# TensorE's sampling program as a loop of two chunks, over a ring of 16 image rows twice, with each step's terms in three parts

## The chip, the cores and the metric

The kernel runs on one core of a Trainium2 chip. The core's engines run side by side and wait for each other through semaphores: TensorE (PE, matmul), VectorE (DVE), ScalarE (ACT), GpSimd (POOL) and SyncE (SP, which here issues nearly all DMAs). The metric is the device time of one execution in microseconds (us), lower is better. Before the change the median of 3 runs is 777.53 us (776.26 to 784.17).

## What is computed

A first layer (channel norm, three 1x1 convolutions, windowed attention, a gate, a residual) ahead of a deformable 3x3 convolution with batch norm, relu and residual, all in fp32 on an array of 8 x 16 x 64 x 64. The change is in the second layer alone:

```python
om = conv3x3(x, w_off) + b_off               # 27 channels
off_y, off_x, mask = om[:, :9], om[:, 9:18], sigmoid(om[:, 18:])
py = off_y + row + ky;  px = off_x + column + kx      # for each of 9 taps
sampled = bilinear(x, py, px) * mask         # zero outside the image
out = einsum("bckhw,ock->bohw", sampled, w) + b
out = relu(batchnorm(out)) + x
```

## The kernel before, in words

The bilinear sample is written as two hat functions. `img4` holds the image already multiplied by each tap's weights: for a column on the partitions, 9 taps x rows x 16 outputs. A matmul with the hat of the horizontal distance as its weights (`wt`, 64 x 64 for one row and tap) picks the columns; a product with the hat of the vertical distance (`aw`) over NR = 7 rows around the pixel and a sum over 9 x 7 = 63 terms pick the rows. Rare larger offsets go another way, that the change does not alter in kind.

Two images lie side by side on the 128 partitions, so the 8 images are PAIRS = 4 passes g over NCH = 8 chunks c of 8 image rows: 32 chunks s, each of SPC = 4 steps, 128 steps n in all, two output rows a step. A step runs through all engines:

- SP loads px of the step, for the chunk ahead, from a scratch array in DRAM, the same 4,608 bytes to 64 partitions and twice (`load_px`, 288 KB each); it waits for `wt_ready` of the step whose place is overwritten.
- ScalarE makes Abs and Relu of it (`hats`) into one of two halves of `wt`.
- TensorE does 40 matmul calls of 64 x 64 (`taps`), in two halves of 512 and 496 columns (32 and 31 of the 63 terms) into 6 of the 8 PSUM banks, two a half, three deep. Each call of an fp32 matmul is two weight loads and two matmuls in the trace.
- VectorE multiplies each half with `aw` (`product`, L886), and sums what is left two steps later (`add`, L897).
- GpSimd folds the 63 terms to 23 (L595, L598), and prepares `aw` (L557, L565) once a chunk.

Between the steps, four times a chunk, stand smaller jobs of TensorE: in rounds of 3, 3 and 2 rows the weighted image rows of the next pass (`slot_round`, read out by ScalarE in `slots_out`), and in the first 16 chunks the offsets of the other pairs (`offsets` at the even chunks, `to_samples` at the odd ones; VectorE's `coordinates` and `peak` belong to them). `img4` holds all 64 rows and a border; a round for chunk s writes the rows that the pass before has done with, so the first pass's rows (7 chunks, `first`) are made ahead of the loop, while offsets of the first pairs are computed.

All programs are written out: TensorE's 32 chunks stand one behind the other, 6,083 matmul calls from the end of the attention loop to the end. The attention stage of the first layer is a loop on TensorE of two times four steps, run three times.

## Time and profile before

| | us |
|---|---|
| median of 3 runs | 777.53 |
| the profiled execution | 782.31 |
| its span, first to last instruction | 780.5 |
| sampling loop, first product to last | 471 |
| share busy: TensorE, its weight loads, VectorE, ScalarE, GpSimd | 79%, 60%, 75%, 66%, 66% |
| moved by DMA | 93.08 MB, 119 GB/s in the mean |

How the rows further down are read: PE is TensorE's matmuls, PEld its weight loads, L with a number a line of the kernel. Busy time is in us with the number of instructions behind it; a few per cent of the matmul records are missing. In a row of waits, "A <- B: 53.2, 38, 3.6" says that A stood idle 53.2 us in 38 pieces of up to 3.6 us until B was done; "issue" is idle time in which nothing that the profile shows was waited for. In a window's row the mean granted share of TensorE's clock (1.00 is 2.4 GHz) stands behind the engines, then the mean busy share of the 16 DMA engines, then GB/s.

### The profile page before, as it was taken

To read this page: it belongs to the slowest core of one execution; us is meant where nothing else is said; L and a number is where in the kernel's file an instruction comes from. 1 tells how busy PE (TensorE), PEld (TensorE's weight loads), DVE (VectorE), ACT (ScalarE), POOL (GpSimd) and SP (SyncE) were. 2 spreads that over 40 slices of the span, in tenths; PEclk is the share of its full clock that TensorE was granted. 3 is DMA by queue.
4 is the path that set the end of the run, shared out by engine and by line. 5 is a ranking of instruction groups with operands and counts; after the bars stand their busy time and mean duration, and the time that the engine had idled before them with its cause. 6 is when DMAs were issued, how large, how long until landed. Compare 5 with 4: busy or idle time off the path is not lost. (4 is left out here: it accounts for less than half of the span.)

```text
span 780.5 us, 31804 instructions
## 1 busy us (share of the span) xinstructions
PE 616.7 (79%) x13528; PEld 466.2 (60%) x13528; DVE 585.8 (75%) x782; ACT 518.3 (66%) x826; POOL 511.7 (66%) x469
## 2 busy tenths in 40 slices
PE   4989999996899898897798688778877767677632
PEld 1335666664345576776676666667766657576532
DVE  3477877786422287998988798889998889879935
ACT  2656676675123596977877687859878687768514
POOL 4036444551331088998979798969989898889920
PEclk9999999998799998999999999999999998879956
DMA  4000000000166277877868676737658878967102
GB/s 180 1 0 2 1 1 0 0 0 2 43 147 146 61 193 186 201 177 187 202 153 199 146 186 156 184 99 190 180 135 190 196 151 174 204 161 191 36 3 107
DMA packets 41747, 93.08 MB, mean 119 GB/s; under 512 B 21647, under 2 KB 21775, under 8 KB 41360
## 3 DMA queue, kind: packets, MB, share of 16 engines
q1 hardware_dynamic: 39762, 90.58, 47.6%
q8 instruction: 104, 1.70, 1.0%
q10 hardware_dynamic: 1854, 0.58, 0.3%
q14 instruction: 27, 0.22, 0.1%
HBM read 79.47 MB, written 3.28 MB: 106 GB/s over the span
## 5 line engine op out<-in xcount | busy, mean ns | idle before, releaser
L1300 PE MATMUL PS<-region 64*64 64x112 f32 (+5 forms) x11184 | 393.5, 268 | 90.0 <-issue 63.5
L1300 PEld LDWEIGHTS PS<-region 64*64 64x64 f32 (+2 forms) x11184 | 314.9, 141 | 138.2 <-issue 97.5
L886 DVE TENSOR_TENSOR region<-PS,region 128x1024 f32<-128x1024 f32 (+1 forms) x256 | 298.9, 1203 | 57.8 <-PE PS L1300 53.2
L595 POOL TENSOR_TENSOR region<-region 128x960 f32<-128x960 f32 x128 | 239.8, 1873 | 50.2 <-DVE region L886 50.0
L1148 ACT ACTIVATE region<-region 128x1152 f32<-128x1152 f32 x128 | 149.1, 1165 | 53.8 <-PE PS L1300 44.3
L1145 ACT ACTIVATE region<-region,cst 128x1152 f32<-128x1152 f32 x128 | 159.3, 1245 | 7.1 <-DMA region<-px_scratch 7.1
L598 POOL TENSOR_TENSOR region<-region 128x320 f32<-128x320 f32 x128 | 117.5, 918 | 10.0
L897 DVE TENSOR_REDUCE region<-region 128x32 f32<-128x736 f32 x128 | 116.2, 908 | 0.0
L1300 PE MATMUL PS<-wg,xp 64*64 64x144 f32 x1024 | 82.7, 291 | 8.9 <-issue 5.9
L1300 PEld LDWEIGHTS PS<-wg,xp 64*64 64x64 f32 x1024 | 64.6, 137 | 17.9 <-issue 12.3
L518 POOL TENSOR_TENSOR region<-region,cst 128x512 f32<-128x512 f32 x32 | 33.8, 1056 | 63.3 <-PE PS L1387 58.7
L1164 ACT ACTIVATE region<-PS 128x432 f32<-128x432 f32 (+1 forms) x75 | 35.6, 479 | 39.9 <-PE PS L1300 39.8
L557 POOL TENSOR_TENSOR region<-x,cst 128x504 f32<-128x504 f32 x32 | 34.3, 1071 | 28.3 <-ACT region L1262 16.3
L1072 ACT ACTIVATE region<-PS 128x512 f32<-128x512 f32 x32 | 19.1, 596 | 35.9 <-PE PS L1395 35.9
L565 POOL TENSOR_TENSOR region<-region 128x504 f32<-128x504 f32 x32 | 34.0, 1061 | 11.1 <-ACT region L1183 11.1
L1300 PE MATMUL PS<-region,woff 96*64 96x512 f32 x120 | 33.2, 595 | 1.5 <-DVE xp L824 0.8
L716 DVE RECIPROCAL region<-PS 128x16 f32<-128x16 f32 x32 | 8.3, 258 | 30.2 <-PE PS L1300 30.2
L1253 ACT ACTIVATE region<-PS 128x432 f32<-128x432 f32 (+1 forms) x21 | 10.3, 490 | 28.7 <-PE PS L1300 28.2
L743 DVE SCALAR_TENSOR_TENSOR PS<-region,wr,PS 128x504 f32<-128x504 f32 (+3 forms) x40 | 29.0, 725 | 0.0
L1395 PEld LDWEIGHTS PS<-cst,region 128*128 128x128 f32 x160 | 16.9, 140 | 18.4 <-issue 14.2
L1395 PE MATMUL PS<-cst,region 128*128 128x128 f32 x160 | 24.3, 282 | 2.6 <-ACT region L1078 2.1
L1300 PE MATMUL PS<-region,bd 128*128 128x512 f32 x48 | 24.0, 624 | 1.1 <-ACT region L1034 1.0
(141 smaller groups left out, 655.2 us busy)
## 6 DMA issues: line engine op xcount, KB each, us to landing
region<-px_scratch SPq DMA_DIRECT2D x256, 288.0 KB, 4.9
out<-region SPq DMA_DIRECT2D x4, 512.0 KB, 3.0
cst<-in_consts SPq DMA_DIRECT2D x1, 1102.5 KB, 8.7
x<-in_x SPq DMA_DIRECT2D x1, 1024.0 KB, 10.7
two<-xp SPq DMA_DIRECT2D x14, 64.0 KB, 3.4
px_scratch<-two SPq DMA_DIRECT2D x48, 18.0 KB
...
```

Source lines behind the costliest of these rows:

```text
L518: pool.tensor_tensor(ks[:, u, :, 0:4 * K1].rearrange("p w (b k) -> p w b k", b=4), kw[:, bass.ds(n * 2 * K1, 2 * K1)].rearrange("p (w k) - ...
L557: pool.tensor_tensor(aw4[:, rows], py4[:, rows, bass.ds(g, 1), :].rearrange("p r g k -> p (r g) k").unsqueeze(3).to_broadcast([P, RPC, KK, ...
L565: pool.tensor_tensor(aw4[:, rows], aw4[:, rows], mk4[:, rows, bass.ds(g, 1), :].rearrange("p r g k -> p (r g) k").unsqueeze(3).to_broadcas ...
L595: pool.tensor_tensor(two_rows[:, :, :, 0:NA - FOLD], two_rows[:, :, :, 0:NA - FOLD], two_rows[:, :, :, FOLD:NA], ALU.add).then_inc(half_re ...
L598: pool.tensor_tensor(two_rows[:, :, :, 0:FOLD - KEEP], two_rows[:, :, :, 0:FOLD - KEEP], two_rows[:, :, :, KEEP:FOLD], ALU.add).then_inc(f ...
L886: v.tensor_tensor(uu[:, 2 * u:2 * u + 2, :, lo:hi], PS[:, banks:banks + 2, 0:(hi - lo) * C].rearrange("p h (a o) -> p h o a", o=C), awf[:, ...
L897: v.tensor_reduce(totals(2 * (n % STEPS), n // STEPS), uu[:, b:b + 2, :, 0:KEEP], AX.X, ALU.add).then_inc(os_ready, 1)
L1145: a.activation(rows, rows, ACT.Abs, bias=c_("negx")).then_inc(ab_ready, 1)
L1148: a.activation(wt[:, i % 2].rearrange("p q k s -> p (q k s)"), rows, ACT.Relu, bias=1.0, scale=-1.0).then_inc(wt_ready, 1)
L1164: a.activation(img4[:, :, bass.ds(slot, ROUNDS[b]), :].rearrange("p k r o -> p r k o"), PS[:, bank, 0:KK * C * ROUNDS[b]].rearrange("p (r ...
L1300: return nc.tensor.matmul(o, l, r, start=start, stop=stop)
L1395: ins = nc.tensor.transpose(PS[:, 6, P * t:P * (t + 1)] if t < 4 else PS[:, 7, 0:P], ee[:, u, P * t:P * (t + 1)], ident)
```

## The change

- TensorE's program of the sampling stage becomes two loops whose body is two chunks, over chunks 0 to 15 (with `offsets` and `to_samples` in it) and 20 to 27. Chunks 16 to 19 and 28 to 31 stay written out. Semaphore values that depend on the chunk come from registers (`turn` adds to a semaphore that nobody waits for).
- So that addresses in the body are constants, the image rows are a ring: two buffers of 16 rows (`RING`), of which a chunk reads one. `img4` is laid out by rows, then taps. The last 8 rows of a chunk's buffer are the first 8 of the next: SP copies them (`share_rows`, 576 KB a chunk); at the start of a pass they come from rows kept apart (`FIRSTS`).
- The inputs of the row rounds are copied to fixed places too: 8 rows of `xp` (264 KB) and one pass's weights (72 KB), `copy_rows`. Rounds now run in 31 chunks, before in 25. Ahead of the loop, `first` runs for 5 chunks in place of 7.
- The 63 terms are three parts of three taps each (`PARTS`), 36 calls and three products of 21 terms a step, each part in its own two banks: one step deep.
- The input of `offsets` in the loop and its output's place have one buffer each instead of two.

```diff
-HALVES = (0, CH // C, NA)
-FOLD = HALVES[1] + 1
+PARTS = tuple(range(0, NA + 1, 3 * NR))
+FOLD = (NA + 3) // 2
...
-        img4 = img.rearrange("p (k r o) -> p k r o", k=KK, o=C)
+        imgf = img.rearrange("p (r a) -> p r a", a=KK * C)
+        img4 = img.rearrange("p (r k o) -> p k r o", k=KK, o=C)
+        xr = [img[:, (FIRSTS + 3 * RPC) * KK * C + u * RPC * (W + 2):][:, 0:RPC * (W + 2)].rearrange("p (r c) -> p r c", c=W + 2) for u in range(2)]
...
         def slot_bank(s, b):
 
-            return (6, 6, 7)[b] if s < AHEAD + 4 else 6 + (s + b) % 2
+            return 7 if s >= PAIRS * NCH - 4 else (6, 6, 7)[b]
...
+            def copy_rows(s):
+
+                if s >= 2:
+                    sp.wait_ge(slot_ready, done(3 * (s - 2) + 2))
+                a = ((s + 1) % NCH * RPC + RPC + XPAD - TOP) * (W + 2)
+                sp.dma_start(xr[s % 2].rearrange("p r c -> p (r c)"), xp[:, a:a + RPC * (W + 2)]).then_inc(xr_in[s % 2], 16)
+                sp.dma_start(wgr[:, s % 2, :], wg[:, (s + 1) // NCH, :]).then_inc(xr_in[s % 2], 16)
...
+                if s == AHEAD - 1:
+                    sp.wait_ge(px_stored[0], stored_by(2 * NCH - 1))
                 for line in range(0, RPC, GR):
                     sp.wait_ge(wt_ready, done(s * SPC + line // GR))
                     load_px(g, c * RPC + line, line, px_in)
+                    if line == GR:
+                        share_rows(s)
+                        if s + 1 < PAIRS * NCH - 1:
+                            copy_rows(s + 1)
+
+            def share_rows(s):
+
+                src, dst = FIRSTS + RPC * (s // NCH), RING + 2 * RPC * ((s + 1) % 2)
+                if s % NCH < NCH - 1:
+                    src = RING + 2 * RPC * (s % 2) + RPC
+                if s >= 1:
+                    sp.wait_ge(row_out, done(3 * s - 1))
+                sp.wait_ge(fi_out, 3 * 4 + 5)
+                sp.wait_ge(t_ready, 3 + 3 * SPC * s)
+                sp.dma_start(imgf[:, dst:dst + RPC, :].rearrange("p r a -> p (r a)"), imgf[:, src:src + RPC, :].rearrange("p r a -> p (r a)")).then_inc(shared_in[s % 2], 16)
...
@@ -882,7 +918,7 @@
 
             def product(m, banks, line, u, ready):
 
-                lo, hi = HALVES[m], HALVES[m + 1]
+                lo, hi = PARTS[m], PARTS[m + 1]
                 v.tensor_tensor(
...
-                for m in range(2):
-                    q = 2 * n + m
-                    dve.wait_ge(t_ready, q + 4)
-                    product(m, 2 * (q % 3), 2 * (n % STEPS), n % UB, u_ready)
+                for m in range(3):
+                    dve.wait_ge(t_ready, 3 * n + m + 4)
+                    product(m, 2 * m, 2 * (n % STEPS), n % UB, u_ready)
...
-                first, end = (isinstance(c, int) and c == e for e in (0, NCH - 1))
-                slot = TOP + H - RPC if first else c * RPC + TOP - RPC
+                end = c == NCH - 1
+                slot = RING + 2 * RPC * ((s + 1) % 2) + RPC
                 for i in range(SPC):
                     hats(s * SPC + i, i, s + 1)
-                    if i in (1, 3) and (first or not last):
+                    if i in (1, 3) and not (last and end):
                         b = i // 2
+                        act.wait_ge(t_ready, 3 + 3 * SPC * s)
+                        act.wait_ge(shared_in[(s + 1) % 2], 16 * (s // 2 + 1))
                         slots_out(3 * s + b, slot + 3 * b, b, slot_bank(s, b))
...
                 if n >= 1:
-                    first(n - 1)
+                    if n <= 5:
+                        first(n - 1)
                     if n >= 3:
                         pe.wait_ge(mk_out, done(n - 3))
-                    to_samples(n - 1, 4 + (n - 1) % 2)
...
-                spans = [(k, 0, NR) for k in range(cut_tap)] + [(cut_tap, 0, cut_row)] if m == 0 else [(cut_tap, cut_row, NR)] + [(k, 0, NR) for k in range(cut_tap + 1, KK)]
-                for k, a, b in spans:
-                    at = (k * NR + a - HALVES[m]) * C
+                for k in range(3 * m, 3 * m + 3):
+                    at = (k * NR - PARTS[m]) * C
                     for h, q in ((0, 0), (1, 1), (0, 1), (1, 0)):
                         image, row = slice(W * h, W * (h + 1)), slice(W * q, W * (q + 1))
-                        ins = mm(PS[row, banks + h, at:at + (b - a) * C], wt[image, u, q, k, :], rows_of(k, q, a, b)[image])
+                        ins = mm(PS[row, banks + h, at:at + NR * C], wt[image, u, q, k, :], rows_of(k, q)[image])
                 return ins
...
+            def between_in_loop(n, u):
+
+                if u == 0:
+                    pe.wait_ge(few_in, 16 * 6 * (n + 1))
+                    turn(n)
+                    offsets(7, xs_few, 0)
+                else:
+                    to_samples(n + NCH, 7, 0)
...
-            for s in range(PAIRS * NCH):
-                g, c, u = s // NCH, s % NCH, s % 2
-                here = c == 0 or g < PAIRS - 1
+            def step_taps(n, e, i):
+
+                pe.wait_ge(wt_ready, done(n))
+                for m in range(3):
+                    pe.wait_ge(u_ready, n * 3 + m + 1)
+                    turn(n)
+                    taps(m, 2 * m, i % 2, lambda k, q: rows_from(RING + 2 * RPC * e + 2 * i + q + k // 3, k)).then_inc(t_ready, 1)
+
+            def rows_from(first_row, k):
+                return img4[:, k, first_row:first_row + NR, :]
+
+            def next_rows(s, j, e, b, bank):
+
+                if b == 0:
+                    pe.wait_ge(xr_in[e], j * 32 + 32)
+                slot_round(3 * s + b, e, b, bank)
+
+            def rows_in(s, j, e):
+
+                pe.wait_ge(row_out, done(3 * s - 1))
+                pe.wait_ge(shared_in[1 - e], j * 16 + 16)
+
+            def two_chunks(j, offsets_too):
+
+                for e in range(2):
+                    s = 2 * j + e
+                    rows_in(s, j, e)
+                    for i in range(SPC):
+                        if i != 1:
+                            b = (0, None, 1, 2)[i]
+                            if b == 1:
+                                pe.wait_ge(row_out, done(3 * s))
+                            if b == 2 and offsets_too:
+                                pe.wait_ge((om_out, mk_out)[e], done(j + NCH))
+                            next_rows(s, j, e, b, slot_bank(0, b))
+                        elif offsets_too:
+                            between_in_loop(j, e)
+                        step_taps(s * SPC + i, e, i)
+
...
-                    n, y = s * SPC + i, c * RPC + 2 * i
-                    pe.wait_ge(wt_ready, done(n))
-                    for m in range(2):
-                        r = 2 * n + m
-                        pe.wait_ge(u_ready, r + 1)
-                        taps(m, 2 * (r % 3), i % 2, lambda k, q, a, b: img4[:, k, y + q + k // 3 + a:y + q + k // 3 + b, :]).then_inc(t_ready, 1)
+                    step_taps(s * SPC + i, s % 2, i)
+
+            with pe.Fori(0, AHEAD // 2) as j:
+                two_chunks(j, True)
+            for s in range(AHEAD, AHEAD + 4):
+                chunk(s)
+            with pe.Fori(AHEAD // 2 + 2, PAIRS * NCH // 2 - 2) as j:
+                two_chunks(j, False)
+            for s in range(PAIRS * NCH - 4, PAIRS * NCH):
+                chunk(s)
```

On TensorE, a row round and a step in the first pass of the kernel before (`region` holds the weighted rows, the hats and more):

```order
L1300 MATMUL PS<-wg,xp 64x144 [waits row_out]
L1300 MATMUL PS<-wg,xp 64x144 x5
L1300 MATMUL PS<-region 64x112 [waits u_ready,wt_ready]
L1300 MATMUL PS<-region 64x112 x15
L1300 MATMUL PS<-region 64x64 x4
L1300 MATMUL PS<-region 64x48 [waits u_ready]
L1300 MATMUL PS<-region 64x48 x3
L1300 MATMUL PS<-region 64x112 x16
```

The same place in the loop of the changed kernel, from the loop's first instruction:

```order
L1710 ISA
L1671 ISA [waits row_out]
L1665 ISA [waits shared_in1]
L1337 MATMUL PS<-region 64x144 [waits xr_in0]
L1337 MATMUL PS<-region 64x144 x5
L1653 ISA
L1655 ISA [waits wt_ready]
L1337 MATMUL PS<-region 64x112 [waits u_ready]
L1337 MATMUL PS<-region 64x112 x11
L1655 REGISTER_ALU
L1337 MATMUL PS<-region 64x112 [waits u_ready]
L1337 MATMUL PS<-region 64x112 x11
```

The two halves with their cut tap (64 and 48 columns) have become parts of 12 calls, each behind a register instruction, and the round, which read `wg` and `xp`, reads copies and waits for them and for the shared rows.

On SP, one chunk's loads of the kernel before, `load_next` of chunk 1, and then the first of the next chunk:

```order
L394 DMA region<-px_scratch 64x1152 [waits wt_ready]
L394 DMA region<-px_scratch 64x1152
L394 DMA region<-px_scratch 64x1152 [waits wt_ready]
L394 DMA region<-px_scratch 64x1152
L394 DMA region<-px_scratch 64x1152 [waits wt_ready]
L394 DMA region<-px_scratch 64x1152
L394 DMA region<-px_scratch 64x1152 [waits wt_ready]
L394 DMA region<-px_scratch 64x1152
L394 DMA region<-px_scratch 64x1152 [waits wt_ready]
```

The same chunk's in the changed kernel:

```order
L411 DMA region<-px_scratch 64x1152 [waits wt_ready]
L411 DMA region<-px_scratch 64x1152
L411 DMA region<-px_scratch 64x1152 [waits wt_ready]
L411 DMA region<-px_scratch 64x1152
L452 DMA region<-region 128x1152 [waits t_ready,fi_out,row_out]
L405 DMA region<-xp 128x528 [waits slot_ready]
L406 DMA region<-wg 128x144
L411 DMA region<-px_scratch 64x1152 [waits wt_ready]
L411 DMA region<-px_scratch 64x1152
L411 DMA region<-px_scratch 64x1152 [waits wt_ready]
L411 DMA region<-px_scratch 64x1152
```

Three copies, two of them behind waits of their own, now stand between the loads of lines 2 and 4.

## Rows read from the trace of the kernel before

**Rows 1.** Windows by stage; busy PE, PEld, DVE, ACT, POOL, clock, DMA, GB/s

```profile
271.80:509.60 237.80, 196.78 (x5869) 166.44 (x5865) 206.99 (x207) 189.41 (x228) 206.75 (x158) 0.96 0.75 180
509.60:571.00 61.40, 48.02 (x1485) 39.84 (x1477) 57.38 (x59) 48.29 (x55) 53.65 (x42) 0.97 0.64 164
571.00:687.20 116.20, 83.17 (x2661) 77.77 (x2665) 101.58 (x98) 89.12 (x97) 103.74 (x80) 0.89 0.78 174
687.20:743.00 55.80, 39.58 (x1384) 36.38 (x1377) 50.87 (x49) 34.84 (x34) 49.41 (x38) 0.90 0.47 121
```

**Rows 2.** Waits, 271.8 to 743 us: us, times, longest

```profile
PEld PS L1300 <- issue: 105.5, 99, 5.0
PE PS L1300 <- issue: 70.4, 48, 4.3
DVE region L886 <- PE PS L1300: 53.2, 38, 3.6
POOL region L595 <- DVE region L886: 50.0, 44, 5.1
```

**Rows 3.** Timeline, 431 to 435 us: start, duration, what, [idle before]

```profile
431.06 0.14 PEld L1300 LDWEIGHTS PS<-region 64*64 64x64 f32 x4 [2.08 <-issue]
...
431.54 1.19 DVE L886 TENSOR_TENSOR region<-PS,region 128x992 f32<-128x992 f32 x1 [0.62 <-PE PS L1300]
...
434.79 2.00 PE L1300 MATMUL PS<-region 64*64 64x112 f32 x80
```

**Rows 4.** The page: engines; DMA queue (packets, MB, share)

```profile
PE 616.7 (79%) x13528; PEld 466.2 (60%) x13528; DVE 585.8 (75%) x782; ACT 518.3 (66%) x826; POOL 511.7 (66%) x469
...
q8 instruction: 104, 1.70, 1.0%
```

**Rows 5.** timeline of DVE from 317 us

```profile
317.01 2.32 DVE L886 TENSOR_TENSOR region<-PS,region 128x1024 f32<-128x1024 f32 x2
319.25 0.91 DVE L897 TENSOR_REDUCE region<-region 128x32 f32<-128x736 f32 x1
320.19 2.32 DVE L886 TENSOR_TENSOR region<-PS,region 128x1024 f32<-128x1024 f32 x2
```

**Rows 6.** timeline of POOL from 316 us

```profile
316.17 1.90 POOL L595 TENSOR_TENSOR region<-region 128x960 f32<-128x960 f32 x1 [0.30 <-DVE region L886]
...
329.53 1.89 POOL L595 TENSOR_TENSOR region<-region 128x960 f32<-128x960 f32 x1
```

**Rows 7.** windows of the attention loop's second and third round

```profile
105.30:137.60 32.30, 30.71 (x320) 20.35 (x318) 25.38 (x61) 22.58 (x78) 15.91 (x25) 1.00 0.00 0
137.60:170.00 32.40, 30.82 (x321) 20.45 (x319) 25.49 (x61) 22.67 (x78) 16.01 (x25) 1.00 0.00 0
```

**Rows 8.** timeline of PE in the attention loop

```profile
104.83 0.30 PE L1414 MATMUL PS<-cst,region 128*128 128x128 f32 x1 [0.51 <-ACT region L1073]
105.07 1.71 PE L1300 MATMUL PS<-region 128*64 128x32 f32 x24
```

**Rows 9.** timeline ahead of the sampling loop, PE

```profile
235.21 2.29 PE L1300 MATMUL PS<-wg,xp 64*64 64x144 f32 x32
...
238.22 2.75 PE L1300 MATMUL PS<-region,woff 96*64 96x512 f32 x12
...
240.89 2.29 PE L1300 MATMUL PS<-wg,xp 64*64 64x144 f32 x32
```

**Rows 10.** groups by line: busy us, mean ns | idle before

```profile
L886 DVE TENSOR_TENSOR region<-PS,region 128x1024 f32<-128x1024 f32 (+1 forms) x256 | 298.9, 1203 | 57.8 <-PE PS L1300 53.2
...
L708 DVE TENSOR_TENSOR region<-PS,region 128x512 f32<-128x512 f32 x32 | 22.1, 692 | 1.7
```

**Rows 11.** windows with DMA near its limit

```profile
8.00:14.00 6.00, 4.72 (x21) 1.36 (x20) 1.81 (x3) 1.26 (x2) 1.83 (x5) 1.00 0.69 290
212.00:223.00 11.00, 10.32 (x25) 4.25 (x23) 4.43 (x8) 2.75 (x4) 5.07 (x4) 1.00 0.74 166
434.00:442.00 8.00, 4.49 (x154) 4.23 (x155) 7.17 (x7) 5.82 (x8) 7.76 (x7) 1.00 0.98 230
```

131 lines of the change are left out of this document (68 added, 63 removed).

## The prediction

> **What bounds the kernel now.** I read the time by stage first. The sampling loop of 128 steps (32 chunks of 4 steps) takes 471 of the 780.5 us. Its first 16 chunks take 237.8 us (14.86 each), the next 4 61.4 us, the next 8 116.2 us (14.53 each), the last 4 55.8 us [rows 1]. No engine is full: VectorE is busy for 207 of the first 237.8 us, GpSimd as long, TensorE 197, ScalarE 189, and the DMA engines 75% of their time.
>
> Then the waits of that stage: VectorE waits 53.2 us for TensorE, GpSimd 50.0 us for VectorE, and TensorE itself 70.4 us for nothing that the profile shows ("issue", 48 times, up to 4.3 us) [rows 2]. So TensorE holds VectorE up, and what holds TensorE up is no engine. The timeline shows it: TensorE stands for 2.08 us with "issue" as the cause, and just behind it VectorE's next product waits 0.62 us [rows 3]. The candidate is code: 104 packets of 16 KB came through the queue of kind "instruction" [rows 4], and TensorE has by far the longest program. TensorE's weight-load queue waits 99 times in this stage, 105.5 us in all, the longest 5.0 [rows 2]: about one wait for each block.
>
> Last, what a chunk costs where nothing waits. VectorE: pair of products 2.24 us (317.01 to 319.25), sum 0.94 us, a step 3.18 us, a chunk of four 12.7 us [rows 5]. GpSimd: 13.36 us from one chunk's first fold to the next one's, with no idle time in it (316.17 to 329.53) [rows 6]. With no waits for TensorE, 13.4 us a chunk is therefore what the other engines need, 1.1 to 1.5 us less than now.
>
> **The change, part by part.**
>
> *The loop.* A step is 36 calls in place of 40; each call is two weight loads and two matmuls in the trace (80 matmuls are 2.00 us, so 72 are 1.80) [rows 3]. The body of the first loop is 334 calls and 75 other instructions, 1,411 instructions. A block of 16 KB is about 256 instructions (an estimate: 104 blocks [rows 4] against 27,056 instructions that the trace has of TensorE's two queues [rows 4]), so the body is 5.5 blocks. Does it stay in the engine's memory? The attention loop is a body of 874 instructions, 3.4 blocks, run three times; its second and third round (32.3 and 32.4 us, 320 and 321 matmuls on record) show a DMA share of 0.00 and 0 GB/s [rows 7]. So a body of 3.4 blocks is kept. A body of 5.5 is not shown; I take it as kept. Then the 24 looped chunks lose their fetch waits. The 8 chunks outside keep them.
>
> The Trainium skill ("Runtime: NRT & Kernel Launch", Instruction fetch mechanics) gives TensorE an instruction memory of 128 KB, which would hold this body, but also says that the memory is only two lines of 16 KB and that a taken branch out of that window forces a fetch. By this second rule the attention loop too would fetch in each round; the trace disagrees, with a DMA share of 0.00 over 65 us. By the first the sum is the one below, by the second the fourth rival's.
>
> *Register waits.* In the loop each of a step's four waits needs its value from a register. The nearest row: in the attention loop a transpose starts at 104.83, and behind a register wait the next matmul at 105.07, 0.24 us on [rows 8]; lower end nothing, since issuing runs ahead of the array. TensorE's step at present prices is 1.80 + 0.52 (32 matmuls of 144 columns a chunk, from 2.29 us for 32 [rows 9], less their tail) + 0.34 (offsets, 2.75 us once in two chunks [rows 9]) = 2.66 us against 3.4. I take 0.1 us a wait, 3.06 us: hidden in the step. All exposed it is 3.6 us (third rival).
>
> *Three parts.* VectorE gets three products of 672 elements in place of 1024 and 992. Slope: 1203 ns for 1008 elements on average against 692 ns for 512, 1.03 ns an element [rows 10]. A product back to back takes 1.12 us [rows 5], so 0.08 us of it is fixed; the third adds 0.08 us a step, 0.3 us a chunk (if nothing overlapped, 0.165 us a step, 0.7 a chunk). VectorE's chunk is 13.0 us, and 13.5 in the first 16 chunks, which hold one 0.74 us and one 0.31 us operation in each two chunks. The total of 10 us is paid only where VectorE sets the pace. TensorE may be one step ahead instead of one and a half; between the end of a product and the next use of its bank lie 2.5 us (two products and a sum), and a part needs 0.6 us, so this costs nothing unless offsets (2.75 us) lie between, 8 times.
>
> *The ring and its copies.* Per chunk SP issues three more DMAs: 8 shared rows (576 KB), 8 rows of xp (264 KB), one group of weights (72 KB), together 0.93 MB. They stand on SP behind the waits for line 2 of the chunk. What each waits for (the step before the chunk done, the last row round out) is then already past, so the loads of lines 4 and 6 behind them are not held. They are issued four steps, some 13 us, ahead of their use. So it is throughput, not latency, that counts. Now DMA work is 0.75 x 237.8 / 16 = 11.15 us a chunk, and 0.78 x 116.2 / 8 = 11.3 us in chunks 20 to 27 [rows 1]. Price of the added bytes: SBUF to SBUF copies from and to 32 partitions moved 166 GB/s at 0.74 busy, 224 GB/s when full; the loads of x over 128 partitions 290 at 0.69, 420 full [rows 11]. That is 4.2 or 2.2 us a chunk. I take 2.7: the new copies are SBUF to SBUF, but span 128 partitions, like x. Less 0.2 for instruction packets no longer moved (104 of them are 1.0% of the span [rows 4], 0.075 us each, three a chunk): 13.65 and 13.8 us a chunk. Loads now run in bursts near their limit (230 GB/s at 0.98 busy [rows 11]), so I add 0.2 us for queueing: 13.9 and 14.0. It is more than VectorE's 13.5 and GpSimd's 13.4, so these, with code loading gone, are what DMA allows.
>
> *First rows.* Rounds for image rows go from 7 chunks to 5 before the loop. An iteration there is 5.69 us, TensorE without a gap (235.21 to 240.89), 2.29 us of it the rounds [rows 9]. Two fall away: 4.6 us, less 0.4 since the last products' latency is uncovered: -4.2.
>
> *Added rounds.* Six more chunks have row rounds, 3 of them in the last four, where TensorE has 16 idle us of 55.8 [rows 1]: hidden. There VectorE's third product shows: +1.3 us. In chunks 16 to 19 (no loop) fewer instructions and one more product cancel.
>
> **The sum.** -4.2 - 16 x (14.86 - 13.9) = -15.4; chunks 16 to 19: 0; 8 x (14.53 - 14.0) = -4.2; +1.3. Together -22.5 us. The profiled execution took 782.3 us (span 780.5), so 759.8 for it; the median of the runs is 777.5, and I predict 755.
>
> **The rivals.**
>
> 1. DMA is no bound, copies at 420 GB/s: 13.5 and 13.4 us a chunk, -21.8 and -9, total -34: 744 us. For it: x's rows. Against: the present loads reach only 235.
>
> 2. DMA takes the gain: copies at 224 GB/s, 15.2 and 15.3 us a chunk: +5.4 + 6.2 - 4.2 + 1.3 = +9: 786 us. It decides from 3.7 us a chunk for the copies on; then the fetch waits are only replaced by ScalarE's waits for px.
>
> 3. Register waits fully exposed: TensorE 3.6 us a step in the first 16 chunks, 14.5 us a chunk: -6 there, -4 in the second loop, -4 before, +1: 765 us, and with the clock down to 0.89, as in chunks 20 to 27 [rows 1], or an exposed wait somewhat dearer, 770 to 777. For it: the values of all four waits now come from registers in each step. Against: the step has 0.8 us to spare.
>
> 4. The body does not stay: each of the 12 rounds waits for code, and block waits remain. The longest wait for issue was 5.0 us, the mean 1.1 [rows 2]; 53.2 of 70.4 us reached VectorE, three quarters. 12 x 5.0 x 0.75 = 45, 12 x 1.1 x 0.75 = 10; plus up to 10 for the third product, less 4: 793 to 828, say 810. This is the Trainium skill's rule ("Runtime: NRT & Kernel Launch", Instruction fetch mechanics) at work.
>
> **How the numbers follow.** Forecast 0.47 (748 to 767), rival 1 0.20, rival 2 0.14, rival 3 0.07, rival 4 0.12. Leaving out the slowest tenth and the fastest corner: 740 to 792. A measurement of this kernel tells about 1% from no change, that is 769.8 to 785.3. Faster: forecast, rival 1 and a sliver of 3, 0.68; within 1%: half of 2 and the rest of 3, 0.14; slower: 4 and the rest of 2, 0.18.
>
> **What would show it.** Right: TensorE's "issue" waits gone from the looped chunks and still there in 16 to 19 and 28 to 31, packets of kind instruction down from 104 to about 45; VectorE's wait for TensorE under 25 us; DMA share 0.9 or more at 220 to 235 GB/s; stage before the loop about 4 us shorter. Wrong: instruction packets in each round of the loop (rival 4); ScalarE's Abs waiting tens of us for px (rival 2); TensorE's gaps spread over all steps (rival 3); DMA share under 0.85 at 13.5 us a chunk (rival 1).

## The result and the profile after

The changed kernel takes 798.50 us (median of 4 runs, 798.11 to 800.86), against 780.54 for the kernel before (median of 4): a ratio of 1.024, 95% interval 1.017 to 1.031. It is slower by 2.4%, where 755 us had been forecast, and it lies 6.5 us above the top of the range. The profiled executions have spans of 796.7 and 780.5 us.

The page of the changed kernel (engines; all DMA packets; the queue for instructions):

```profile
PE 640.0 (80%) x12632; PEld 474.0 (59%) x12632; DVE 594.9 (75%) x910; ACT 523.4 (66%) x838; POOL 511.9 (64%) x469
...
DMA packets 55083, 121.10 MB, mean 152 GB/s; under 512 B 23135, under 2 KB 27231, under 8 KB 54752
...
q8 instruction: 45, 0.74, 0.4%
```

Instruction packets fell from 104 to 45 [rows 4], as forecast; the bytes rose from 93 to 121 MB. Its windows by stage, columns as in [rows 1], with the first 16 chunks in two pieces (chunks 0 and 1, the first round of the loop; chunks 2 to 15), and chunks 20 to 27 also in two (20 and 21, the first round of the second loop; 22 to 27):

```profile
269.50:308.30 38.80, 26.96 (x678) 23.42 (x674) 25.24 (x33) 25.89 (x32) 24.22 (x18) 0.88 0.81 204
308.30:506.70 198.40, 178.99 (x4717) 142.44 (x4710) 185.82 (x238) 163.65 (x196) 182.11 (x141) 0.98 0.99 247
506.70:574.40 67.70, 47.97 (x1282) 41.14 (x1278) 58.88 (x76) 47.32 (x54) 54.18 (x42) 0.90 0.87 209
574.40:697.60 123.20, 96.49 (x2573) 85.40 (x2567) 103.89 (x130) 92.50 (x106) 104.19 (x80) 0.89 0.91 218
...
574.40:607.40 33.00, 24.59 (x639) 22.32 (x635) 26.23 (x33) 21.16 (x24) 25.07 (x20) 0.84 0.81 195
607.40:697.60 90.20, 71.89 (x1944) 63.08 (x1938) 77.66 (x97) 71.34 (x83) 79.12 (x61) 0.91 0.94 227
...
697.60:760.40 62.80, 42.69 (x1354) 39.25 (x1346) 53.41 (x66) 40.28 (x45) 50.15 (x39) 0.94 0.65 161
```

Chunks 2 to 15 take 14.17 us each at a DMA share of 0.99: there the loop gives nearly what was forecast. The rest of the sampling stage became slower: the first round (38.8 us for two chunks), the two stretches that are written out, and also chunks 20 to 27, which are a loop.

The packet records of the traces say where TensorE's code was fetched. Instruction packets of q8 by the start of VectorE's products:

| | ahead of 0 | 0, 1 | 2-15 | 16-19 | 20, 21 | 22-27 | 28-31 | behind |
|---|---|---|---|---|---|---|---|---|
| before | 11 | 6 | 40 | 12 | 4 | 16 | 13 | 2 |
| after | 10 | 6 | 0 | 10 | 5 | 0 | 12 | 2 |

So both loops fetch in their first round and in no other. In chunks 22 to 27 all 16 packets are gone, and the stretch takes 90.1 us where it took 90.6. What holds it up there can't be code. The waits from 269.5 to 760 us, columns as in [rows 2]:

```profile
PEld PS L1337 <- issue: 129.7, 140, 6.0
DVE region L922 <- PE PS L1337: 62.6, 57, 5.0
PE PS L1337 <- issue: 45.5, 24, 5.8
PE PS L1337 <- DMA region<-wg: 18.9, 10, 3.2
```

TensorE's own waits for "issue" halved in number (48 to 24) but the longest grew from 4.3 to 5.8 us, and VectorE waits 62.6 us for TensorE, before 53.2 [rows 2]. A wait is new: TensorE for the DMA copies of the row rounds' inputs. In chunks 2 to 15, where no code is fetched, TensorE's matmuls never wait for "issue", but its weight loads do:

```profile
PEld PS L1337 <- issue: 42.7, 78, 2.6
```

So these waits of the weight loads are mostly not waits for blocks; the 48 and 24 waits of the matmuls are the better sign. Of the 48 in the kernel before, 17 (46.5 of 70.4 us) end 1.25 to 1.66 us behind the end of an instruction packet that landed during the wait; in the changed kernel 12 of 24 do (35.3 of 45.5 us), 1.34 to 1.68 us behind it. The timeline of the first round (TensorE's second chunk, then VectorE) shows what such a wait costs now, against the 2.08 us of [rows 3]:

```profile
293.76 3.87 PE L1337 MATMUL PS<-region 64*64 64x144 f32 x122 [3.51 <-issue]
303.39 4.95 PE L1337 MATMUL PS<-region 64*64 64x112 f32 x84 [5.76 <-issue]
...
304.48 0.86 DVE L922 TENSOR_TENSOR region<-PS,region 128x672 f32<-128x672 f32 x1 [5.01 <-PE PS L1337]
```

And the loads take longer to land (DMA issues: count, size, median us from issue to landing):

```profile
region<-px_scratch SPq DMA_DIRECT2D x256, 288.0 KB, 6.6
region<-region SPq DMA_DIRECT2D x31, 576.0 KB, 7.0
```

The same rows of the kernel before:

```profile
region<-px_scratch SPq DMA_DIRECT2D x256, 288.0 KB, 4.9
```

A load of px took 4.9 us from issue to landing, now 6.6. If an instruction block is slowed likewise, each block that TensorE still waits for comes later. That is Theory A of the experiments: **the copies load the DMA engines, and the blocks that are still fetched come later for it.** One part of it the profile doesn't show: the transfer of a block by itself took about 1.2 us on average in both kernels. If blocks come later, they begin later; when a block is asked for is in no trace.

SyncE changed too. Its own waits in chunks 20 to 27, before (571 to 687.2 us) and after (574.4 to 697.6):

```profile
SPq L394 <- ACT region L1148: 19.3, 13, 3.4
...
SPq L411 <- ACT region L1183: 4.6, 4, 2.4
```

In chunks 20 to 26 SP issues 18 DMAs a chunk in the changed kernel, before 15: eight loads of px, seven for the rare offsets, and now three copies. It is without a wait for 118.6 of 123.2 us there, before for 96.9 of 116.2.

The table reads every kernel of this study alike: us from VectorE's first product to its last, by chunks, then the span, VectorE's wait for TensorE from the first product on (a row of the waits), and the span less that wait.

| kernel | first product | 0, 1 | 2-15 | 16-19 | 20-27 | 28-31 | span | DVE<-PE | rest |
|---|---|---|---|---|---|---|---|---|---|
| before | 271.8 | 29.4 | 208.3 | 61.4 | 116.2 | 54.8 | 780.5 | 53.2 | 727.3 |
| after | 269.5 | 38.7 | 198.5 | 67.6 | 123.2 | 60.5 | 796.7 | 62.6 | 734.1 |
| e1 after, written out | 267.6 | 29.9 | 233.8 | 66.0 | 132.0 | 61.6 | 828.7 | 96.1 | 732.6 |
| e2 after, copies of 8 KB | 267.7 | 33.1 | 190.7 | 63.6 | 114.8 | 55.9 | 763.7 | 34.5 | 729.2 |
| e3 before, three parts | 271.0 | 27.1 | 206.3 | 61.6 | 116.9 | 52.6 | 773.3 | 40.3 | 733.0 |
| e6 before, more copies | 273.8 | 29.9 | 221.7 | 65.7 | 121.7 | 58.2 | 808.3 | 81.2 | 727.1 |
| e4 after, rows by ScalarE | 269.6 | 31.0 | 191.1 | 63.7 | 112.7 | 57.3 | 762.6 | 31.6 | 731.0 |
| e5 e4, few copies | 267.8 | 30.0 | 190.6 | 62.0 | 110.2 | 57.1 | 755.1 | 26.5 | 728.6 |
| e8 e4, fewer and earlier copies | 267.1 | 30.2 | 190.9 | 61.9 | 112.6 | 56.0 | 756.7 | 27.8 | 728.9 |
| e10 e4, 576 KB dummy | 268.0 | 36.4 | 195.6 | 65.2 | 124.1 | 58.4 | 785.1 | 54.7 | 730.4 |
| e9 e4, 2 x 264 KB dummy | 272.6 | 30.1 | 195.8 | 62.8 | 122.0 | 60.4 | 780.8 | 47.3 | 733.5 |
| e11 dummy in chunks 2-13 only | 271.4 | 31.9 | 192.7 | 62.3 | 113.2 | 55.1 | 763.9 | 31.5 | 732.4 |
| e12 after, loop from chunk 2 | 267.3 | 30.7 | 208.9 | 65.5 | 126.7 | 61.2 | 797.9 | 67.5 | 730.4 |
| e7 after, body of four chunks | 269.4 | 34.0 | 267.2 | 63.7 | 146.9 | 59.2 | 878.4 | 144.7 | 733.7 |

The last column is the finding that orders the others. Over spans from 755 to 878 us it stays between 727 and 734, 727 for the two kernels with two products a step and 729 to 734 for those with three: nearly all of what the variants gain and lose is VectorE waiting for TensorE. It doesn't say what TensorE waited for. Each row is one traced execution. The ratios below are to the kernel before as it was timed beside each group.

### The profile page after: what moved, and what is told of

Same layout as the page of the kernel before. It is cut to its first block and busy times, and to the rows that moved or that the text cites. A ratio compares the mean times of both kernels' runs of the same rounds, so it can differ in the third digit from the quotient of the medians.

```text
span 796.7 us, 31101 instructions
## 1 busy us (share of the span) xinstructions
PE 640.0 (80%) x12632; PEld 474.0 (59%) x12632; DVE 594.9 (75%) x910; ACT 523.4 (66%) x838; POOL 511.9 (64%) x469
## 5 line engine op out<-in xcount | busy, mean ns | idle before, releaser
L1337 PE MATMUL PS<-region 64*64 64x112 f32 (+4 forms) x11152 | 448.4, 281 | 90.8 <-issue 43.4
L1337 PEld LDWEIGHTS PS<-region 64*64 64x64 f32 (+2 forms) x11152 | 363.9, 141 | 155.8 <-issue 129.6
L922 DVE TENSOR_TENSOR region<-PS,region 128x672 f32<-128x672 f32 x384 | 308.5, 851 | 67.0 <-PE PS L1337 62.6
L1183 ACT ACTIVATE region<-region 128x1152 f32<-128x1152 f32 x128 | 149.1, 1165 | 38.6 <-PE PS L1337 28.2
L1432 PEld LDWEIGHTS PS<-cst,region 128*128 128x128 f32 x160 | 16.9, 140 | 18.5 <-issue 14.2
L1337 PE MATMUL PS<-two,bd 128*128 128x512 f32 x48 | 24.0, 661 | 1.8 <-DVE two L855 1.1
L531 POOL COPY region<-region 128x32 f32<-128x32 f32 x8 | 2.3, 291 | 35.7 <-ACT region L1063 35.7
L883 DVE SCALAR_TENSOR_TENSOR two<-PS,bcol,cst 128x512 f32<-128x512 f32 x16 | 11.9, 746 | 16.4 <-PE PS L1337 16.4
L740 DVE TENSOR_REDUCE region<-PS 128x8 f32<-128x512 f32 x32 | 21.8, 680 | 2.3 <-PE PS L1337 2.3
```

What stands on the lines that cost most here:

```text
L922: v.tensor_tensor(uu[:, 2 * u:2 * u + 2, :, lo:hi], PS[:, banks:banks + 2, 0:(hi - lo) * C].rearrange("p h (a o) -> p h o a", o=C), awf[:, ...
L1183: a.activation(wt[:, i % 2].rearrange("p q k s -> p (q k s)"), rows, ACT.Relu, bias=1.0, scale=-1.0).then_inc(wt_ready, 1)
L1337: return nc.tensor.matmul(o, l, r, start=start, stop=stop)
L1432: ins = nc.tensor.transpose(PS[:, 6, P * t:P * (t + 1)] if t < 4 else PS[:, 7, 0:P], ee[:, u, P * t:P * (t + 1)], ident)
```

## The experiments

Beside the first four the kernel before took 779.4 us.

**e1, the loops written out.** All of the change except the loops: the same body as plain code.

```diff
-            with pe.Fori(0, AHEAD // 2) as j:
+            for j in range(AHEAD // 2):
                 two_chunks(j, True)
...
-            with pe.Fori(AHEAD // 2 + 2, PAIRS * NCH // 2 - 2) as j:
+            for j in range(AHEAD // 2 + 2, PAIRS * NCH // 2 - 2):
                 two_chunks(j, False)
```

> The changed kernel with both loops of TensorE written out again (all 32 chunks one behind the other), nothing else undone. Theory A (the added copies make each wait for a block of instructions longer, and the loops save what they can): the 24 looped chunks go to the pace of the written-out chunks 16 to 19, 16.9 us, so about 237 to 270 and 123 to 135 us: 835 to 850 us. Theory B (the loop itself costs: register waits, back edges): 798 us or less, about 785.

Measured: 828.87 us, 1.067 times the kernel before (1.054 to 1.081), with 97 instruction packets. So the loops save 30 us (34 by the ratios); the rest of the change costs 50. Theory A's side, though the number came out below its range. Waits from 267.6 to 792 us:

```profile
PEld PS L1337 <- issue: 159.5, 156, 5.2
DVE region L922 <- PE PS L1337: 96.1, 69, 6.3
PE PS L1337 <- issue: 71.9, 47, 4.9
```

TensorE waited 70.4 us in 48 pieces for issue before [rows 2] and 71.9 in 47 here; what grew is the weight loads' waiting (105.5 to 159.5) and what of all of it reaches VectorE (53.2 to 96.1). Part of the first growth isn't code: in chunks 2 to 15 the weight loads have 82 such waits here and 78 in the changed kernel, which fetches nothing there. Of the matmuls' waits 21 (54.4 us) end 1.3 to 1.8 us behind a packet.

**e2, small copies.** The changed kernel with the three copies cut to 16 elements a partition from the third chunk on, so most of the shared rows and of the rounds' inputs is stale there.

```diff
-                sp.dma_start(xr[s % 2].rearrange("p r c -> p (r c)"), xp[:, a:a + RPC * (W + 2)]).then_inc(xr_in[s % 2], 16)
+                n, m = (RPC * (W + 2), KK * C) if s < 2 else (16, 16)
+                sp.dma_start(xr[s % 2].rearrange("p r c -> p (r c)")[:, 0:n], xp[:, a:a + n]).then_inc(xr_in[s % 2], 16)
...
+                few_or_all = RPC * KK * C if s < 2 else 16
```

> The changed kernel with its three copies a chunk cut to 16 elements a partition from chunk 2 on, so the image rows, input rows and weights are stale there; all waits and issues stay. Theory A: DMA load falls back to that of the kernel before, waits for instruction blocks to about 1.1 us each, looped chunks to 13.5 us: 750 to 762 us. Theory B (loop, register waits or the ring's tight waits cost): 785 us or more.

Measured: 766.28 us, 0.987 (0.982 to 0.992). The bytes of the copies cost 32 us (28 by the ratios). Issues, waits and loops are those of the changed kernel, with 45 packets again, so this is the cleanest test of the bytes; the windows of chunks 2 to 15 and 20 to 27:

```profile
300.80:491.50 190.70, 176.82 (x4706) 138.88 (x4698) 185.38 (x239) 163.69 (x197) 182.87 (x141) 1.00 0.83 194
...
555.10:669.80 114.70, 90.44 (x2546) 79.25 (x2550) 103.41 (x128) 91.86 (x104) 103.59 (x80) 0.94 0.80 169
```

**e3, three parts alone**, in the kernel before (`PARTS` for `HALVES`, three waits and products a step, nothing else).

> The kernel before with the three parts of three taps alone. Theory A: one more product is 0.08 us a step, 10 us if VectorE always set the pace, against a tenth fewer matmul instructions and so about 94 blocks in place of 104: 775 to 790 us. Theory C (the parts, one step deep, are what slowed the changed kernel): 795 us or more.

Measured: 778.45 us, 1.001 (0.996 to 1.007). The parts, with 96 instruction packets in place of 104, cost nothing that can be told. That clears the third product and the shallower banks, as far as this kernel goes. In the table VectorE waits 13 us less for TensorE in this kernel (40.3 for 53.2) and the rest is 6 us longer: the third product mostly fills waiting time.

**e6, more copies alone**, in the kernel before: three dummy DMAs a chunk with the bytes of the change's copies, at their place in SP's program.

```diff
+                    if line == GR:
+                        for a, b in ((0, 1152), (1152, 1680), (1680, 1824)):
+                            sp.dma_start(spare[s, :, a:b], xp[:, a:b]).then_inc(spared, 16)
```

> The kernel before with three DMAs a chunk added at the place on SP where the changed kernel has its copies, of the same sizes (576, 264 and 72 KB), from SBUF to a spare array in DRAM; nobody waits for them but the end. Theory A: 99 waits for instruction blocks grow from 1.1 to about 1.6 us, and most of it reaches VectorE: 800 to 830 us, DMA share about 0.9. Rival (DMA load alone is harmless, it is the ring's waits): 778 to 786 us.

Measured: 816.08 us, 1.055 (1.041 to 1.070), with the same 104 packets as before. Copies that no work waits for cost 37 us (43 by the ratio) where TensorE fetches all its code. Waits from 273.8 to 773 us:

```profile
DVE region L892 <- PE PS L1306: 81.2, 53, 3.8
...
ACT region L1151 <- DMA region<-px_scratch: 25.1, 16, 3.7
```

Here ScalarE waits 25.1 us for px too (7.1 in the kernel before, 0.3 in the changed one). So part of the 37 us may be late px loads and not late code: 21.8 of the 25.1 us lie in chunks 20 to 27, where SP itself waits only 2.1 us (before 19.3) and so issues late. The matmuls' waits behind a packet hardly changed, 50.8 us in 18 pieces for 46.5 in 17. This run shows what the copies cost, not that code is the way.

Beside the next four the kernel before took 783.4 us.

**e4, the shared rows by ScalarE.** The largest copy goes from the DMA engines to ScalarE, 1.15 us a chunk there.

```diff
-                        share_rows(s)
...
+                    if i == 1 and not (last and end):
+                        act.wait_ge(t_ready, 3 + 3 * SPC * s)
+                        if s:
+                            act.wait_ge(row_out, done(3 * s - 1))
+                        act.wait_ge(shared_in[(s + 1) % 2], s // 2 + 1)
...
+                        a.activation(imgf[:, dst:dst + RPC, :].rearrange("p r a -> p (r a)"), imgf[:, src:src + RPC, :].rearrange("p r a -> p (r a)"), ACT.Copy).then_inc(shared_in[s % 2], 1)
```

> The kernel after with one edit: the copy of a chunk's last 16 rows to the other buffer (576 KB, the largest of the three copies) is made by ScalarE, as one Copy of 128x1152, and SP's DMA for it is gone. The other two copies (72 KB and 264 KB) stay. Theory A (the copies load the DMA engines, and each instruction block that PE and PEld wait for comes later for it, above all in a loop's first round and in the chunks that are written out): most of what the run with small copies gained over the kernel after (798.5 to 766.3, so 32 us for 0.91 MB a chunk) comes back, in proportion to the bytes 0.63 x 32 = 20 us, to 778; the range is 770 to 787, the DMA share of the whole of the chunks under 0.9. Rival D (ScalarE, which now does 1 us more a chunk on the path to the next chunk's products, takes the gain): 790 or more, with PE or VectorE waiting for ScalarE in the looped chunks by over 10 us in all.

Measured: 762.19 us, 0.974 (0.967 to 0.982), faster than both kernels and below Theory A's 770 to 787. ScalarE's extra work does not show (rival D out). Windows of chunks 0 and 1, 2 to 15, 16 to 19, 20 to 27, and 22 to 27 alone:

```profile
269.60:300.60 31.00, 25.00 (x680) 21.16 (x676) 25.10 (x33) 28.17 (x34) 24.24 (x18) 0.94 0.89 210
300.60:491.60 191.00, 176.69 (x4718) 139.05 (x4710) 185.28 (x238) 177.41 (x209) 181.93 (x141) 1.00 0.94 217
491.60:555.30 63.70, 48.04 (x1288) 39.23 (x1288) 58.37 (x75) 51.85 (x60) 54.12 (x42) 0.92 0.72 179
555.30:668.00 112.70, 92.53 (x2544) 80.38 (x2548) 103.27 (x129) 99.64 (x112) 103.44 (x80) 0.92 0.88 196
...
585.00:668.00 83.00, 69.85 (x1946) 59.85 (x1943) 77.52 (x96) 74.35 (x84) 75.42 (x58) 0.95 0.94 207
```

The timeline of TensorE in the first round, at the two places shown above for the changed kernel, has 1.04 and 2.74 us where that had 3.51 and 5.76:

```profile
289.67 3.87 PE L1332 MATMUL PS<-region 64*64 64x144 f32 x122 [1.04 <-issue]
296.28 4.96 PE L1332 MATMUL PS<-region 64*64 64x112 f32 x109 [2.74 <-issue]
```

TensorE's program and its 45 blocks are the same, and no row of the changed kernel has an engine waiting for the copy that went; but TensorE waits less for them: 5 waits of the matmuls (10.9 us) end behind a packet, for 12 (35.3 us) there. Its waits from 269.6 to 727 us:

```profile
PEld PS L1332 <- issue: 102.0, 138, 6.2
DVE region L910 <- PE PS L1332: 31.6, 36, 3.7
PE PS L1332 <- issue: 18.7, 14, 2.7
PE PS L1332 <- DMA region<-wg: 11.2, 7, 3.8
```

Taking away the other two copies as well (e2) brings no more: 763.7 us of span against 762.6. The cost is not in proportion to the bytes.

Where the gain lies is as telling. Of the 32.7 us by which e4's sampling stage is shorter than the changed kernel's, 14.8 lie in chunks 0 and 1, 16 to 19 and 28 to 31, where code is fetched. 7.4 lie in chunks 2 to 15, where none is. And 10.5 lie in chunks 20 to 27, only 3.4 of them in the round that fetches (33.1 to 29.6 us) and 7.1 in chunks 22 to 27 (90.1 to 83.0 us). So late blocks can be at most 18.2 of the 32.7 us that this copy costs.

**e5, few copies.** e4, and the 72 KB of weights are copied only where the pass changes.

```diff
+                if s < 2 or (s + 1) // NCH != (s - 1) // NCH:
                     sp.dma_start(wgr[:, s % 2, :], wg[:, (s + 1) // NCH, :]).then_inc(xr_in[s % 2], 16)
+                else:
+                    sp.sem_inc(xr_in[s % 2], 16)
```

> The kernel before this one (the copy of 16 rows on ScalarE) with one more edit: the 72 KB copy of wg is issued only where the pass changes, since the ring's slot of that parity holds it already. Theory A: 72 KB a chunk less of DMA, 0.05 x 32 = about 2 us, and one SP issue a chunk less in chunks 20 to 26, where copies were issued late, another 1 to 4 us: 772, range 764 to 780. Rival E (neither the bytes nor the issue of this small copy matter): within 2 us of the kernel with ScalarE's copy.

Measured: 760.27 us, 0.976 (0.968 to 0.985), which can't be told from e4, and below Theory A's range. Inconclusive between the two.

**e8, early copies.** e5, and `copy_rows(s + 1)` is issued ahead of the chunk's loads.

> The kernel before this one with one more edit: the 264 KB copy of the x rows (with the semaphore of wg) is issued at the start of a chunk's loads instead of behind its seventh row's. Theory A with its second part (in chunks 20 to 26 SP issues the gather's and the image's loads with no pause between, so that copies behind them land late, and PE waits for them, 10.7 to 13.3 us in chunks 20 to 27 of the two traces): the waits of PE for a DMA copy from wg or x fall under 4 us in chunks 20 to 27, and the kernel takes 764, range 756 to 774, faster than the kernel before the change by 1 to 3%. Rival F (the loads now behind the copies land late in their place): VectorE waits for the image's rows or gather's data by as much, and the time stays within 2 us of the kernel with few copies, or above.

Measured: 757.15 us, 0.969 (0.961 to 0.976): the fastest kernel of the study, but within the intervals of e4 and e5. A wait of TensorE in chunks 20 to 27 (555.3 to 668) in e4:

```profile
PE PS L1332 <- DMA region<-wg: 10.5, 6, 3.8
```

and in e8 (550.1 to 662.7):

```profile
PE PS L1334 <- ACT region L1173: 14.8, 14, 2.1
```

The wait for the copies is gone, and 14.8 us of waiting for ScalarE's hats stands there instead. The hats need the px loads, which are now behind the copies, but ScalarE itself waits only 3.2 us for px there, so why they are late is not shown. Chunks 20 to 27 take 112.7 us in e4, 110.2 in e5 and 112.6 in e8. So the wait moved, though to another engine than rival F named, and the stage kept its length.

**e7, a body of four chunks.** 11 blocks instead of 5.5, with 4 and 2 rounds.

```diff
-            with pe.Fori(0, AHEAD // 2) as j:
-                two_chunks(j, True)
+            with pe.Fori(0, AHEAD // 4) as q:
+                two_chunks(2 * q, True)
+                two_chunks(2 * q + 1, True)
```

> The kernel after with loops whose body is four chunks (2,822 instructions of PE, 11 blocks of 16 KB) with 4 and 2 rounds in place of 8 and 4 rounds of two chunks (5.5 blocks). Nothing else changes. Theory A (a body is kept only if it fits what the engine holds, which two chunks' 5.5 blocks do; four chunks' 11 may not): not kept, some 97 packets of instructions, and the time of the written-out form, 822 to 835. Rival G (a body of 11 blocks is kept too): the first round of each loop fetches, chunks 0 to 3 and 20 to 23, so 24 less 8 chunks are without fetches, some 52 to 58 packets, and the time is 800 to 812.

Measured: 882.03 us, 1.124 (1.112 to 1.136). The page and the waits (269.4 to 842 us):

```profile
q8 instruction: 107, 1.75, 0.9%
...
PEld PS L1337 <- issue: 190.8, 140, 8.5
DVE region L922 <- PE PS L1337: 144.7, 96, 9.1
PE PS L1337 <- issue: 126.5, 50, 8.3
```

The body is not kept (Theory A's side), but the time is 47 us above its range: a loop whose body is not kept is dearer than the same chunks written out, 301.2 against 263.7 us for chunks 0 to 15, where the wait rows of 0 to 15 name about as many pieces (122 against 116). The issue waits of TensorE's two queues, which overlap, sum to 317 us here and 231 in e1. Of the matmuls' waits 36 (115.4 us) end behind a packet, in e1 21 (54.4 us). The longest waits stand near the start of a round; this one is TensorE's first work of the third:

```profile
414.43 2.08 PE L1337 MATMUL PS<-region 64*64 64x144 f32 x20 [5.39 <-issue]
```

Beside the last four the kernel before took 775.8 us.

**e10, the same bytes as a dummy.** e4, with a DMA of 576 KB that nothing reads at the place where the changed kernel issued `share_rows`.

```diff
                     if line == GR:
+                        for a, b in ((0, 1152),):
+                            sp.dma_start(spare[s, :, a:b], xp[:, a:b]).then_inc(stored, 16)
                         if s + 1 < PAIRS * NCH - 1:
```

> The kernel with ScalarE's copy (e4), and at the place of the removed copy one dummy DMA of 576 KB from SBUF to DRAM that nothing reads: the bytes and the packets (4608 bytes) of the kernel after, but no work waits for them. Theories P and Q (load on the DMA engines): 785 to 802, with waits for instruction blocks of TensorE over 160 us from the first product on. Rival R (the kernel after lost its time since work waited for this copy to land, directly or by its place in a queue that later loads share, and not by load): 758 to 768.

Measured: 787.17 us, 1.0125 (1.006 to 1.019). By the ratios the dummy costs 0.038 of the time before, 30 us, of the 0.050 (39 us) that lie between e4 and the changed kernel. No work waits for the dummy, so rival R is out as the main cause. But the dummy is bytes and one more issue of SP, and this run doesn't part the two. Waits from 268 to 750 us:

```profile
PEld PS L1335 <- issue: 120.5, 139, 4.8
DVE region L913 <- PE PS L1335: 54.7, 49, 4.3
PE PS L1335 <- issue: 26.5, 18, 4.3
PE PS L1335 <- DMA region<-wg: 26.5, 13, 4.1
```

VectorE waits 23.1 us more than in e4, and the span is 22.5 us longer. On TensorE the growth is in two kinds: issue by 7.8 us (weight loads by 18.5) and the copies for the row rounds by 15.3; they stand behind the dummy on SP. Against e4 the stages grow by 5.4 us in chunks 0 and 1, 4.5 in 2 to 15, 1.5 in 16 to 19, 11.4 in 20 to 27 and 1.1 in 28 to 31. The largest growth is again where SP has no time left: 10.6 of the 11.4 lie in chunks 22 to 27 (93.6 for 83.0 us), with one block fetched. The forecast of over 160 us of issue waits was a miss: 147.

**e9, the same load in shorter packets.** As e10, with two dummies of 264 KB (`((0, 528), (528, 1056))`).

> The kernel with ScalarE's copy of the 16 rows (e4, 762.2 us), and in a chunk's loads, where the kernel after issued its 576 KB copy, two dummy DMAs of 264 KB each from SBUF to DRAM that nothing reads: 528 KB a chunk in packets of 2112 bytes. The kernel with small copies and the one with ScalarE's copy took the same time although the second still moves 336 KB a chunk more, so not every byte costs alike. Theory P (what makes the instruction blocks late is the 576 KB copy's packets of 4608 bytes, and copies of shorter packets cost little): 762 to 772. Theory Q (the bytes count, whatever their packets, from the share at which the DMA engines have no slack): 785 to 802, near the kernel after.

Measured: 779.77 us, 1.004 (1.001 to 1.007), between the two theories' ranges. By ratios it costs 0.030 (23 us) against the 30 of the single DMA, for 0.92 of its bytes. So packets of 2112 bytes are not free (Theory P falls); whether they cost less a byte is inside the intervals. One row stands against a simple rule: with 0.92 of e10's added bytes the loop's first round took 30.1 us here (granted clock 1.00) and 36.4 in e10 (0.86). Each is one trace. Whether the lower clock is a cause or a result of TensorE's waiting there, no run tells.

**e11, the dummy only where nothing is fetched**: in chunks 2 to 13.

```diff
+                        for a, b in ((0, 1152),) if 2 <= s < AHEAD - 2 else ():
+                            sp.dma_start(spare[s, :, a:b], xp[:, a:b]).then_inc(stored, 16)
```

> As the kernel with the dummy of 576 KB a chunk, but the dummies are issued in chunks 2 to 13 alone, where TensorE runs a body that it holds and fetches nothing. Theory A (load costs only where instruction blocks are fetched): 760 to 768, chunks 2 to 15 at 13.6 to 13.9 us each with a DMA share of 0.95 or more. Rival S (load costs wherever it is, since the image's loads come later): a third or more of the whole dummy's cost, 775 or more, with VectorE or ScalarE waiting for the image's or the weights' loads in chunks 2 to 15.

Measured: 765.18 us, 0.986 (0.979 to 0.992), in Theory A's range. The window of chunks 2 to 15:

```profile
303.20:495.90 192.70, 174.74 (x4716) 138.67 (x4707) 185.35 (x238) 178.48 (x211) 182.94 (x141) 1.00 0.99 251
```

A DMA share of 0.99 at 251 GB/s for 190 us, and the stage is 1.6 us longer than at 0.94 (e4). Twelve of the 31 dummies cost 1.3 us of span, all 31 cost 22.5. Timed side by side, e10 is 22 us slower than e11, for 19 dummies more. Against e4, timed in another group, the twelve cost 3 us by the medians and 9 by the ratios, the latter uncertain by 7. So a dummy is cheaper in these chunks, how much cheaper is less sure than the span says. Chunks 22 to 27, with one block fetched, are not such a place: there e10's six dummies came with 10.6 us.

**e12, the loop begins at chunk 2.** The changed kernel, chunks 0 and 1 written out.

```diff
-            with pe.Fori(0, AHEAD // 2) as j:
+            two_chunks(0, True)
+            with pe.Fori(1, AHEAD // 2) as j:
                 two_chunks(j, True)
```

> The kernel after with chunks 0 and 1 written out ahead of the first loop, which then has 7 rounds (chunks 2 to 15). Theory L (the first round of a loop, in which its blocks are fetched, costs more than the same chunks written out, 38.8 against 29.8 us for chunks 0 and 1, under this DMA load): chunks 0 and 1 take 29 to 32 us, chunks 2 and 3 take 36 to 40 in place of 28.6, and the time is 797 to 805. Rival M (what was dear was chunks 0 and 1 at that moment, the first chunks with all loads running, and not the loop's first round): chunks 0 and 1 take 36 or more again, or chunks 2 and 3 take under 33, and the time in the second case is 788 to 795.

Measured: 803.87 us, 1.040 (1.033 to 1.046). Windows of chunks 0 and 1, and 2 and 3:

```profile
267.30:298.00 30.70, 24.10 (x677) 20.42 (x671) 25.02 (x32) 25.78 (x33) 23.88 (x18) 0.97 0.94 241
298.00:332.50 34.50, 26.76 (x701) 23.52 (x697) 26.96 (x35) 23.45 (x29) 25.69 (x21) 0.88 0.86 215
```

Written out, chunks 0 and 1 are 8 us shorter than in the loop, and chunks 2 and 3 now pay: 34.5 us, between the 28.4 of two kept chunks (198.5 / 7) and the forecast 36 to 40. The dear stretch moved with the loop's first round (Theory L, at a smaller price than forecast). The first round without the 576 KB copy took 31.0 (e4) and 31.9 (e11), with a dummy 36.4 (e10) and 30.1 (e9). So it is dear in some kernels with the load and in none without. Why fetching inside a loop waits longer than along plain code stays open.

## Why the prediction was wrong

By the prediction's own steps:

| step | forecast, us | measured, us | miss |
|---|---|---|---|
| before the loop | -4.2 | -2.3 | +1.9 |
| chunks 0, 1 | -1.6 | +9.3 | +10.9 |
| chunks 2-15 | -13.8 | -9.8 | +4.0 |
| chunks 16-19 | 0 | +6.2 | +6.2 |
| chunks 20-27 | -4.2 | +7.0 | +11.2 |
| chunks 28-31 | +1.3 | +5.7 | +4.4 |
| sum | -22.5 | +16.1 | +38.6 |

(Forecast for 0, 1: two of sixteen times 13.9 is 27.8 against 29.4 measured before; 2-15 the rest. "Before the loop" compares two traces; the first product starts at a median of 268.0 us over the changed kernel and the ten variants that share its code there, so the -4.2 was about right.)

**The step that failed** is this one: "So it is throughput, not latency, that counts." It was meant for the copies' own landing, and with it the load was priced as time of the DMA engines alone: 2.7 us a chunk that had to fit beside 11.15. Where that is the question, in chunks 2 to 15, the price was good: 14.17 us a chunk for a forecast of 13.9. The engines' share times the length of a chunk was 14.0 us (0.99 x 14.17) for 13.65 worked out. But the load had a second price, which the sum put at nothing. With all issues in place and the bytes gone the kernel takes 28 to 32 us less (e2); with the 576 KB copy gone it takes 36 to 39 us less (e4). px lands in 6.6 us for 4.9, and "The 8 chunks outside keep them" kept the waits for code at their old price: e4 shows chunks 16 to 19 fall from 67.6 to 63.7 us, 28 to 31 from 60.5 to 57.3, and 0 and 1 from 38.7 to 31.0, though the blocks are the same. That late blocks are what these stretches lost is argued from the waits behind packets (35.3 us, in e4 10.9). The three are 14.8 of 32.7 us: the same copy costs 7.4 us in chunks 2 to 15, where nothing is fetched, and 10.5 in chunks 20 to 27.

**A second step** failed in the count: "Then the 24 looped chunks lose their fetch waits." Each loop's first round fetches its blocks, so it is 20 chunks, and the first round cost more than plain code under this load (38.7 against 29.9 us, e1; 34.5 against 28.4, e12). In chunks 0 and 1 this is 8.8 of the 10.9 us of miss, with the doubt that e9 leaves (30.1 us under nearly the same load). Chunks 20 and 21 went from 25.6 to 33.1 us.

**A third** is the largest miss of the table, chunks 20 to 27. "Per chunk SP issues three more DMAs" was priced in bytes alone, the issuing at nothing. SP had waited 19.3 of 116.2 us there and waits 4.6 of 123.2 now. In chunks 22 to 27 the waits for code are gone as forecast, and nothing is gained (90.6 and 90.1 us). e4, with one issue and 576 KB less a chunk, takes 83.0 us there. e2, with all issues and hardly any bytes, takes 87.3, which fits a price for the issue by itself. That SP sets the pace there is read from its waits and these two rows; no run changes the issues alone. It also answers "They are issued four steps, some 13 us, ahead of their use": TensorE waits 18.9 us for the copies, 12.6 of it in chunks 22 to 27. "the loads of lines 4 and 6 behind them are not held" does hold for ScalarE, which waits 0.3 us for px, before 7.1. e8 moves the copies to another place in SP's program without gain, but in a kernel without the 576 KB copy.

A reading failed too, without weight in the sum: "about one wait for each block" took the weight loads' 99 waits for block waits. In chunks 2 to 15 the changed kernel has 78 of them and no block. And "Right" asked for VectorE's wait for TensorE under 25 us; it was 62.6.

**What was right.** The body of 5.5 blocks is kept: 45 packets, as said, and chunks 2 to 15 at 14.17 us. e1 prices the loops at 30 us. The third product costs 0.07 to 0.08 us a step (VectorE's three products and the sum in the kept rounds, timeline of the changed kernel):

```profile
327.04 2.39 DVE L922 TENSOR_TENSOR region<-PS,region 128x672 f32<-128x672 f32 x3
329.34 0.91 DVE L933 TENSOR_REDUCE region<-region 128x32 f32<-128x736 f32 x1
330.29 2.39 DVE L922 TENSOR_TENSOR region<-PS,region 128x672 f32<-128x672 f32 x3
```

A step is 3.25 us (327.04 to 330.29), before 3.18 [rows 5], and e3 finds no cost in the time. Register waits do not show: TensorE's matmuls have no wait for issue in chunks 2 to 15. And what the other engines need was well estimated: with the load gone, e4's chunks 2 to 15 take 13.65 us for the 13.4 to 13.5 worked out.

**The rivals.** Rival 2 ("DMA takes the gain", 786 us) had the right culprit and the wrong mechanism: it expected ScalarE to wait for px and 15.2 us a chunk everywhere; ScalarE waits 0.3 us, and chunks 2 to 15 take 14.17. Rival 4 (the body does not stay) gave a range that holds the measured time, by the wrong cause, since the body stays. It was also too low for what it described: e7, where a body does not stay, took 882 us. The forecast range missed by 6.5 us, but the -22.5 us of its sum and the +16.1 measured differ by 38.6, so it is no near miss. The Trainium skill ("Runtime: NRT & Kernel Launch", Instruction fetch mechanics) gives TensorE 128 KB. The two bodies lie on both sides of it, 5.5 blocks (88 KB) kept and 11 (176 KB) not. The Trainium skill's other rule there, that the memory is two lines of 16 KB, does not fit: by it each round would fetch, and the 45 packets leave none for chunks 2 to 15 and 22 to 27.

**What stays open**: the 9 us by which the changed kernel is slower than e10 (0.050 against 0.038, barely outside what the intervals allow); how the copy's 36 to 39 us divide between late blocks, late copies and SP's issuing; why a first round is dearer than plain code, and what the clock has to do with it; and why 0.33 MB a chunk less (e2 against e4) gained nothing where 0.58 MB gained 36.
